# Two layers of graph, mixture and attention on one core: expert rows gathered by a list made on TensorE, results of the second mixture stored in token order

## The chip, the cores and the metric

The kernel runs on one core of a Trainium2 chip. The metric is the device time of one execution in microseconds (us). The core has five engines with queues of their own: TensorE (PE; PEld is its weight load), VectorE (DVE), ScalarE (ACT), GpSimd (POOL) and SyncE (SP), which here only issues DMAs. They pass work to one another through semaphores.

## The reference

3327 tokens of 256 numbers go through two graph layers, two mixtures of experts and one attention; all of it is in f32.

```python
x = x + _L0_gnn_ref(_layernorm(x), adj, W, b)          # (dis * adj * dis) @ x @ W.T + b
x = x + _L0_ffn_ref(_layernorm(x), gate_w, ..., b2)     # top 2 of 8 experts, weighted by softmax
x = x + _L1_gnn_ref(_layernorm(x), adj, W, b)           # the same with relu
x = x + _L1_ffn_ref(_layernorm(x), ln1_g, ..., b2)      # attention, then the second mixture

def _moe(xf, router_w, router_b, w1, b1, w2, b2):       # in _L1_ffn_ref
    probs = jax.nn.softmax(xf @ router_w + router_b, axis=-1)
    _, topk_idx = jax.lax.top_k(probs, TOP_K)
    capacity = int(np.ceil(T * CAPACITY_FACTOR / N_EXPERTS))
    out = jnp.zeros_like(xf)
    for i in range(N_EXPERTS):
        mask = (topk_idx == i).any(-1)
        sel = jnp.sort(jnp.where(mask, tok, T))[:capacity]
        xi = xf[jnp.minimum(sel, T - 1)]
        hi = jax.nn.gelu(xi @ w1[i] + b1[i], approximate=False)
        yi = hi @ w2[i] + b2[i]
        out = out.at[sel].set(yi, mode='drop')          # the last expert that has the token wins
    return out
```

An expert is a product 256 x 1024, a gelu and a product 1024 x 256. In the first mixture every token has two experts, and their outputs are added by their weights. In the second one a token has the output of at most one expert: of its two the one with the higher number that still has room.

## The kernel before

Tokens lie in 26 tiles of 128 (`NT`, padded to `NP` = 3328 rows); a tile is [128 partitions, 256]. `m.x` and `m.xhat` hold x and its normed form in SBUF for all tiles. Large products take f32 operands as two parts, `_hi` (rounded by ScalarE) and `_lo` (the rest, by VectorE), and three passes of TensorE. The program is a row of stages, each a block of its own in which every engine has a queue written out by hand; a stage ends when all its engines have ended.

1. `graph_layer(first=True)`: 182 pieces of the adjacency matrix, by 7 chunks of columns (`CHUNKS`; the first six are 4 tiles wide, the last one 2). A loop runs over positions g; at each, SP loads a piece into `adj_raw`, ScalarE makes `adj_hi` (L410), VectorE `adj_lo` (L636), TensorE multiplies (L570 to L572). The first four chunks run together up to position 103, the others follow one by one. The tail work of chunk c (product by W, normalisation, later products) is spread over positions counted from `turns[c]`, by lists that `at_positions` makes (L246 to L264): positions stand for time here. POOL fills `slots0` and `slots1` with zeroes (27 DMAs, 13.8 MB) in this layer. PE waits for the parameters before its first product (L552).
2. `mixture`: `mixture_routes` makes for each token and choice a slot (`put`, where its row goes) and `get` (where its result lies); slots of one expert are neighbours, in chunks of 256 (`CHUNK`). `mixture_scatter` (L858) sends the normed rows from SBUF to `slots` in DRAM with one indirect DMA a tile and choice on POOL: 52 in the first mixture, 26 in the second. The stage waits for all of them. `expert_layers` (L872) runs over 34 chunks in the first mixture and 20 in the second. SP loads the chunk's rows (L920), both weight matrices (L922, 1 MB each) and biases two chunks ahead; all engines have loops over pairs of chunks. TensorE transposes the rows of the next chunk in the middle of a chunk (`turn`, L937), when rows and weights have arrived; ScalarE and VectorE split rows, weights and hidden values; POOL stores 256 rows of results (L1040), waits until they have landed, and frees the buffer.
3. `graph_layer(first=False)`: the same with further work in its tail: the results of the first mixture are gathered by POOL (L346) and added to x; x of a chunk is normed at `turns[c]` + 8 to + 10 (`roots`, `applies`), but as ScalarE overwrites x, POOL first stores the unnormed x to `x_kept` in DRAM (`keep`), and ScalarE waits for this store (L428's releaser). The order in POOL's queue is: keep(0), then for each chunk c the output bias of c, keep(c + 1), and the q and k stores of the tiles of c (L340). Second normalisation at + 12 to + 14, transposition at + 12, q and k products of a tile (L546, 16 products) and v (L549) at + 13, copied out of PSUM at + 17 by ScalarE. ScalarE's order within a position is the piece's `adj_hi`, then evacuations, roots, applies, and last `taken` and `copied` (`xt`, L439), for which TensorE waits.
4. `attend`: attention by heads.
5. `second_mixture`: normalisation, x loaded back, `gate_logits` (a transposition and a small product for each tile, `transposed_products`), then `mixture` as above, whose last stage `mixture_gather` (L1046) gathers the result of each token with 26 indirect DMAs on POOL and adds it to x with its weight (L1068, 0 where no expert had room). A last stage stores x to `out` in one DMA of 3.4 MB (L1533).

## Time and profile before

| | us |
|---|---|
| median of 3 runs | 2963.14 (2962.2 to 2964.66) |
| profiled execution | 2960.15 |
| its span in the trace | 2958.5 |
| TensorE busy | 2472.5 (84% of the span) |
| VectorE busy | 1993.0 (67%) |
| ScalarE busy | 1573.0 (53%) |
| POOL busy | 1251.6 (42%) |
| routes of the first mixture end | 393.2 |
| first product of its expert loop, its end | 481.7, 889 |
| second graph layer | 891 to 1325 |
| attention | 1326 to 2504 |
| first product of the second expert loop, its end | 2668.9, 2907 |

The stages follow one another, so a saving within one moves all later ones. An engine's busy share of the whole span mixes stages with different limits: the page's second part, the span in 40 slices of 74 us, shows this.

```profile
PE   4789805999997998758999999999999997409992
DVE  5775424888877865438777777777777773328883
ACT  4554304777764543323666666666666665206761
POOL 0001051000004402234888888888888886230003
PEclk9999957999998999876999999999999999559996
```

A digit is the busy share in tenths. Slice 6 (370 to 444 us) is the routes and the scatter: PE 0, POOL 5. Slices 7 to 12 are the first expert loop, 13 to 18 the second graph layer; slices 35 and 36 (PE 4 and 0) hold gates, routes and scatter of the second mixture, and 37 to 39 its expert loop.

### The profile page before, as it was taken

How to read it: one execution, taken by the hardware profiler on the slowest of the kernel's cores; microseconds unless marked ns; L12 is line 12 of the kernel's file. 1: busy time of each engine (PE TensorE's matmuls, PEld its weight loads, DVE VectorE, ACT ScalarE, POOL GpSimd, SP SyncE). 2: the span in 40 equal slices, each digit the busy share in tenths (PEclk: the TensorE clock that was granted, in tenths of full speed). 3: DMA queues.
4: the chain of work that ended last, by engine and by line, in shares of the span. 5: the costliest groups of instructions: out<-in, count | busy, mean ns of one | idle time of the engine just before them, and what ended most of it. 6: DMA issues, size and time to landing. Idle time of an engine off the chain costs nothing. (4 is left out here: it accounts for less than half of the span.)

```text
span 2958.5 us, 54884 instructions
## 1 busy us (share of the span) xinstructions
PE 2472.5 (84%) x20856; PEld 1919.4 (65%) x20856; DVE 1993.0 (67%) x2987; ACT 1573.0 (53%) x2652; POOL 1251.6 (42%) x738
## 2 busy tenths in 40 slices
PE   4789805999997998758999999999999997409992
PEld 3668704999995877644666666666666664409992
DVE  5775424888877865438777777777777773328883
ACT  4554304777764543323666666666666665206761
POOL 0001051000004402234888888888888886230003
PEclk9999957999998999876999999999999999559996
DMA  9988115666646753224000000220000000126663
GB/s 398 362 309 341 47 67 193 230 229 238 240 162 217 235 185 129 97 90 122 14 16 10 14 16 16 46 48 16 10 14 16 10 12 1 46 83 223 241 232 105
DMA packets 118767, 375.96 MB, mean 127 GB/s; under 512 B 22256, under 2 KB 56432, under 8 KB 100656
## 3 DMA queue, kind: packets, MB, share of 16 engines
q1 hardware_dynamic: 96192, 302.78, 28.9%
q0 software_dynamic: 20800, 65.82, 6.0%
q10 hardware_dynamic: 1584, 4.75, 0.4%
q8 instruction: 129, 2.11, 0.3%
q14 instruction: 62, 0.51, 0.1%
HBM read 314.30 MB, written 58.98 MB: 126 GB/s over the span
## 5 line engine op out<-in xcount | busy, mean ns | idle before, releaser
L1255 POOL TENSOR_TENSOR at_pool_sum<-at_pool_sum,at_probs 128x1024 f32<-128x1024 f32 x364 | 866.7, 2381 | 97.0 <-ACT at_probs L1381 55.7
L1410 DVE TENSOR_REDUCE at_part_max<-ps_x 128x2 f32<-128x1024 f32 x624 | 734.4, 1221 | 228.1 <-PE ps_x L1311 227.8
L1381 ACT ACTIVATE at_probs<-ps_s 128x512 f32<-128x512 f32 x1352 | 698.4, 603 | 323.3 <-PE ps_s L1270 292.8
L1270 PE MATMUL ps_s<-at_qst,at_kst 97*128 97x256 f32 x2704 | 517.6, 311 | 5.2 <-ACT at_probs L1381 4.0
L1270 PEld LDWEIGHTS ps_s<-at_qst,at_kst 97*128 97x128 f32 x2704 | 368.9, 189 | 218.5 <-ACT at_probs L1381 127.2
L1287 PE MATMUL ps_oz<-at_probs,k_xhat 128*32 128x256 f32 (+1 forms) x5408 | 391.4, 386 | 0.0
L570 PE MATMUL ps_acc<-adj_hi,y_hi 128*128 128x512 f32 (+1 forms) x728 | 290.1, 399 | 93.6 <-DMA k_bias<-bias 32.8
L636 DVE TENSOR_TENSOR adj_lo<-adj_raw,adj_hi 128x1024 fp32r<-128x1024 f32 (+1 forms) x182 | 208.7, 1148 | 184.1 <-ACT adj_hi L410 181.7
L1040 POOL DMA_DIRECT2D results<-ex_res x54 | 39.3, 727 | 645.4 <-DVE ex_res L1027 645.4
L571 PE MATMUL ps_acc<-adj_lo,y_hi 128*128 128x512 f32 (+1 forms) x728 | 278.1, 382 | 0.0
L572 PE MATMUL ps_acc<-adj_hi,y_lo 128*128 128x512 f32 (+1 forms) x728 | 277.9, 382 | 0.0
L991 ACT ACTIVATE ex_hid<-ps_ex_h,ex_b 128x256 f32<-128x256 f32 x432 | 197.7, 476 | 128.3 <-PE ps_ex_h L943 115.1
L1009 DVE TENSOR_TENSOR ex_w_lo<-ex_w,ex_w_hi 128x2048 fp32r<-128x2048 f32 x108 | 242.7, 2289 | 33.5 <-ACT ex_w_hi L981 33.5
L941 PE MATMUL ps_ex_h<-ex_rt_hi,ex_w_hi 128*128 128x256 f32 x864 | 246.1, 285 | 9.8 <-DVE ex_w_lo L1009 9.8
L941 PE MATMUL ps_ex_o<-ex_w_hi,ex_hid_hi 128*128 128x256 f32 x864 | 246.7, 286 | 0.0
L943 PE MATMUL ps_ex_h<-ex_rt_hi,ex_w_lo 128*128 128x256 f32 x864 | 243.2, 282 | 0.0
L942 PE MATMUL ps_ex_h<-ex_rt_lo,ex_w_hi 128*128 128x256 f32 x864 | 243.0, 281 | 0.0
L942 PE MATMUL ps_ex_o<-ex_w_lo,ex_hid_hi 128*128 128x256 f32 x864 | 242.4, 281 | 0.0
L943 PE MATMUL ps_ex_o<-ex_w_hi,ex_hid_lo 128*128 128x256 f32 x864 | 242.3, 280 | 0.0
L410 ACT ACTIVATE adj_hi<-adj_raw 128x1024 fp32r<-128x1024 f32 (+1 forms) x182 | 174.9, 988 | 104.4 <-PE ps_acc L572 104.0
L570 PEld LDWEIGHTS ps_acc<-adj_hi,y_hi 128*128 128x128 f32 x728 | 140.6, 193 | 127.9 <-issue 70.5
L1311 PE MATMUL ps_x<-at_keys,at_queries 32*128 32x512 f32 x1248 | 191.0, 509 | 27.3 <-DMA at_keys<-qk_parts 13.2
(201 smaller groups left out, 4047.6 us busy)
## 6 DMA issues: line engine op xcount, KB each, us to landing
ex_w<-w SPq DMA_DIRECT2D x108, 1024.0 KB, 6.8
adj_raw<-adjT SPq DMA_DIRECT2D x156, 512.0 KB, 4.9
k_xhat<-adj SPq DMA_DIRECT2D x26, 1664.0 KB, 8.6
slots<-zeros POOLq DMA_DIRECT2D x27, 512.0 KB, 24.2
ex_rows<-slots SPq DMA_DIRECT2D x54, 256.0 KB, 2.9
results<-ex_res POOLq DMA_DIRECT2D x54, 256.0 KB, 2.8
at_qst<-qk_parts SPq DMA_DIRECT2D x78, 128.0 KB, 2.5
ex_b<-b SPq DMA_DIRECT2D x54, 128.0 KB, 2.1
```

The lines of the kernel that those rows point to most:

```text
L570: pe.matmul(out, y_hi[:, k, cols], hi[:, g % PIECE_RING, at], start=k == 0, stop=False)
L571: pe.matmul(out, y_hi[:, k, cols], lo[:, g % PIECE_RING, at], start=False, stop=False)
L572: last = pe.matmul(out, y_lo[:, k, cols], hi[:, g % PIECE_RING, at], start=False, stop=k == NT - 1)
L941: pe.matmul(out, hi, by_hi, start=start, stop=False)
L942: pe.matmul(out, hi, by_lo, start=False, stop=False)
L943: return pe.matmul(out, lo, by_hi, start=False, stop=stop)
L1009: dve.tensor_tensor(w_lo[:, k, layer, :], w[:, k, layer, :], w_hi[:, k, layer, :].bitcast(F32), ALU.subtract).then_inc(weights_lo, 1)
L1255: pool.tensor_tensor(pool_sum[:, g % 2], pool_sum[:, g % 2], probs[:, tile % RING], ALU.add).then_inc(pool_added, 1)
L1270: last = pe.matmul(ps_s[:, unit % S_BANKS, hh, :], kst[:, 2 * j + hh, k * P:(k + 1) * P], qst[:, g % 2, 2 * j + hh, :], start=True, stop=True)
L1287: last = pe.matmul(ps_oz[h * DK:(h + 1) * DK, 0, :], m.xhat[0:rows, k, (hg * FOUR + h) * DK:(hg * FOUR + h + 1) * DK], probs[0:rows, tile ...
L1381: act.activation(probs[:, tile % RING, 2 * j:2 * j + 2], ps_s[:, unit % S_BANKS], ACT.Exp, scale=scale).then_inc(taken, 1)
L1410: dve.tensor_reduce(part_max[:, g % 2, heads, qt, kc], ps_x[:, pair, :], AX.X, ALU.max).then_inc(x_free, 1)
```

## The change

1. Rows and lists. The normed rows go to DRAM in token order (`rows_d`): in the first layer chunk by chunk on POOL behind `normed`, in the second mixture in one DMA on SP within `transposed_products`. `mixture_scatter`, `slots0`, `slots1` and their zeroes are gone; instead the part of `results1` that holds tokens is zeroed (13 DMAs, 3.4 MB).
2. `expert_layers` first makes a list of the token in each slot. VectorE splits `put` into column (`put >> 7`) and lane (`put & 127`), marks both as one-hot rows of bf16 (`col_hot`, `lane_hot`) in two groups, and multiplies the columns by the tile number; ScalarE scales them by the lane. TensorE sums the products over all marks (`find_rows`: 52 marks and 68 columns for the first mixture, 26 and 40 for the second), which gives the token at each (lane, column). VectorE makes `index` of it (`list_rows`).
3. POOL gathers the rows of a chunk with two indirect DMAs (`fetch`, two chunks ahead of the store) in place of SP's load; `turn` waits only for these rows. SP's weight loads of chunks 0 and 1 wait for counts of `weights_lo` that now come in two steps, the second after the list. POOL's loop is written out.
4. In the second mixture (`SPREAD`) two indirect DMAs store a chunk's results in token order (`place`; slots without a token go to rows of their own). `mixture_gather` and the last stage become `mixture_output`: SP loads the results in 7 groups, VectorE adds, ScalarE stores 7 groups of `out`.
5. Second graph layer: the store of x to `x_kept` goes from POOL to SP, at `turns[c]` + 11, with two semaphores in turn; `applies` is at + 13 and all that follows it three positions later. For both layers ScalarE's `taken` and `copied` come ahead of evacuations, roots and applies within a position, and the roots are numbered by their positions (`norm`). The wait for the parameters goes from TensorE's start to its first product by W.

```diff
+        @block.sync
+        def _(sp):
+            sp.dma_start(rows.rearrange("(k p) d -> p k d", p=P), src[:]).then_inc(rows_kept, 16)
+            sp.wait_ge(rows_kept, 16)
...
-    applies = at_positions([(at + 10 + q, p) for at, c, p, q in pairs])
-    roots2_begin, roots2_end = at_positions([(turns[c] + 12, c) for c in range(CHUNKS)]), at_positions([(turns[c] + 13, c) for c in range(CHUNKS)])
-    applies2 = at_positions([(at + 14 + q, p) for at, c, p, q in pairs])
+    applies = at_positions([(at + (10 if first else 13) + q, p) for at, c, p, q in pairs])
+    keeps = at_positions([(turns[c] + 11, c) for c in range(CHUNKS)])
+    roots2_begin, roots2_end = at_positions([(turns[c] + 15, c) for c in range(CHUNKS)]), at_positions([(turns[c] + 16, c) for c in range(CHUNKS)])
+    applies2 = at_positions([(at + 17 + q, p) for at, c, p, q in pairs])
+    norms = sorted((turns[c] + (15 if second else 8), second, c) for c in range(CHUNKS) for second in range(1 if first else 2))
+    norm = {(c, second): n for n, (_, second, c) in enumerate(norms)}
...
-        turned_at = at_positions([(at + 12 + 3 * q, p) for at, c, p, q in pairs])
-        copied_at = at_positions([(at + 16 + 3 * q, p) for at, c, p, q in pairs])
-        produced_at = at_positions([(at + 13 + 3 * q + i, 2 * p + i) for at, c, p, q in pairs for i in range(2)])
-        taken_at = at_positions([(at + 17 + 3 * q + i, 2 * p + i) for at, c, p, q in pairs for i in range(2)])
-        split_at = at_positions([(at + 18 + 3 * q + i, 2 * p + i) for at, c, p, q in pairs for i in range(2)])
+        turned_at = at_positions([(at + 15 + 3 * q, p) for at, c, p, q in pairs])
+        copied_at = at_positions([(at + 19 + 3 * q, p) for at, c, p, q in pairs])
+        produced_at = at_positions([(at + 16 + 3 * q + i, 2 * p + i) for at, c, p, q in pairs for i in range(2)])
+        taken_at = at_positions([(at + 20 + 3 * q + i, 2 * p + i) for at, c, p, q in pairs for i in range(2)])
+        split_at = at_positions([(at + 21 + 3 * q + i, 2 * p + i) for at, c, p, q in pairs for i in range(2)])
...
-                done = 0
-                for slots, chunks in ((m.slots0, MOE0_CHUNKS), (m.slots1, MOE1_CHUNKS)):
-                    cols = chunks * CHUNK // P * D
-                    view = slots[0:chunks * CHUNK, :].rearrange("(p n) d -> p (n d)", p=P)
-                    for n in range(0, cols, ZERO_COLS):
-                        width = min(ZERO_COLS, cols - n)
-                        pool.dma_start(view[:, n:n + width], zeros[:, 0:width]).then_inc(cleared, 16)
-                        done += 16
-                pool.wait_ge(cleared, done)
+                for n in range(0, NT, ZERO_TILES):
+                    pool.dma_start(m.results1[0:NP, :].rearrange("(p n) d -> p n d", p=P)[:, n:n + ZERO_TILES, :], zeros[:]).then_inc(rows_kept, 16)
+                for c in range(CHUNKS):
+                    at = slice(first_tile(c), first_tile(c + 1))
+                    pool.wait_ge(normed, at.stop)
+                    pool.dma_start(m.rows_d[at.start * P:at.stop * P, :].rearrange("(k p) d -> p k d", p=P), m.xhat[:, at, :]).then_inc(rows_kept, 16)
+                pool.wait_ge(rows_kept, 16 * (CHUNKS + NT // ZERO_TILES))
...
-            keep(0)
             for c in range(CHUNKS):
...
-                if c + 1 < CHUNKS:
-                    keep(c + 1)
...
+            def keep(c):
+                at = slice(first_tile(c), first_tile(c + 1))
+                sp.wait_ge(chain, at.stop)
+                sp.dma_start(m.x_kept[:, at.start * D:at.stop * D], m.x[:, at, :].rearrange("p t d -> p (t d)")).then_inc(x_kept[c % 2], 16)
...
+                if not first:
+                    for c in keeps(g):
+                        keep(c)
...
+                for n in taken_at(g):
+                    take_logits(n) if first else round_product(n)
+                for p in copied_at(g):
+                    copy_turned(p)
...
-                        act.wait_ge(x_kept, 16 * c + 16)
-                        apply(p, m.x, m.x, normed, 2 * c + 1)
+                        act.wait_ge(x_kept[c % 2], c // 2 * 16 + 16)
+                        apply(p, m.x, m.x, normed, norm[c, 0] + 1)
...
+                elif first:
+                    pe.wait_ge(params_loaded, 16 * 7)
...
-                    sp.dma_start(rows[:, k], slots[ds(i * 2 * CHUNK + k * CHUNK, CHUNK), :].rearrange("(a p) d -> p a d", p=P)).then_inc(loaded[k], 16)
...
-            eng.wait_ge(loaded[k], n * 24 + (48 - 24 * k))
+            eng.wait_ge(loaded[k], n * 16 + (32 - 16 * k))
...
+            def find_rows():
+                for i in range(MARKS):
+                    if i % GROUP == 0:
+                        pe.wait_ge(planes_made, i // GROUP + 1)
+                        pe.wait_ge(lanes_made, i // GROUP + 1)
+                    last = pe.matmul(ps_o[:, 0, 0:2 * COLS], lane_hot[:, i, :], planes[:, i].rearrange("p a n -> p (a n)"),
+                                     start=i == 0, stop=i == MARKS - 1)
+                last.then_inc(found, 1)
+
             def turn(n, k):
-                arrived(pe, n, k)
+                pe.wait_ge(rows_come[k], n * 16 + (32 - 16 * k))
...
+            def lanes():
+                for g in range(MARKS // GROUP):
+                    act.wait_ge(matched, g + 1)
+                    at = slice(g * GROUP, (g + 1) * GROUP)
+                    act.activation(planes[:, at, 0, :], col_hot[:, at, :], ACT.Copy, scale=lane[:, 0:1]).then_inc(lanes_made, 1)
+
+            lanes()
...
-            dve.sem_inc(weights_lo, 4)
+            dve.sem_inc(weights_lo, 2)
...
+            def mark_rows():
+                c = Count(coded)
+                put = m.put[:, 0:n_rows, :].rearrange("p a k -> p (a k)")
+                c.inc(dve.tensor_scalar(code_i[:, 0], put, 7, None, ALU.arith_shift_right))
+                c.inc(dve.tensor_scalar(code_i[:, 1], put, P - 1, None, ALU.bitwise_and))
+                c.inc(dve.tensor_scalar(lane[:], m.token_f[:, 0:1], 1.0 if SPREAD else 0.0, None, ALU.add))
+                c.settle(dve)
+                c.inc(dve.tensor_copy(code[:], code_i[:]))
+                c.settle(dve)
+                for g in range(MARKS // GROUP):
+                    at = slice(g * GROUP, (g + 1) * GROUP)
+
+                    def along(a, n):
+                        return a.rearrange("p (i b) -> p i b", b=1).broadcast_to([P, GROUP, n])
+
+                    def numbers(n):
+                        return m.iota_b[:, 0:n].rearrange("p (b n) -> p b n", b=1).broadcast_to([P, GROUP, n])
+
+                    dve.tensor_tensor(col_hot[:, at, :], along(code[:, 0, at], COLS), numbers(COLS), ALU.is_equal).then_inc(matched, 1)
+                    dve.tensor_tensor(lane_hot[:, at, :], along(code[:, 1, at], P), numbers(P), ALU.is_equal)
+                    dve.wait_ge(matched, g + 1)
+                    tile = g * GROUP % NT
+                    dve.tensor_tensor(planes[:, at, 1, :], col_hot[:, at, :], along(m.iota_b[:, tile:tile + GROUP], COLS), ALU.mult).then_inc(planes_made, 1)
+
+            def list_rows():
+                dve.wait_ge(found, 1)
+                dve.tensor_copy(slot_of[:].rearrange("p a n -> p (a n)"), ps_o[:, 0, 0:2 * COLS]).then_inc(coded, 1)
+                dve.wait_ge(coded, 5)
...
+                if not SPREAD:
+                    dve.scalar_tensor_tensor(index[:], slot_of[:, 1], float(P), slot_of[:, 0], ALU.mult, ALU.add).then_inc(listed, 1)
+                    return
...
+                dve.tensor_scalar(index[:], slot_of[:, 0], -1.0, 0.0, ALU.add, ALU.max).then_inc(listed, 1)
...
+                c.inc(dve.scalar_tensor_tensor(place[:], slot_of[:, 0], -1.0, slot_of[:, 1], ALU.add, ALU.add))
...
+            mark_rows()
+            list_rows()
+            dve.sem_inc(weights_lo, 2)
...
+            def fetch(n):
+                if n >= 2:
+                    pool.wait_ge(turned, n - 1)
+                for a in range(TT):
+                    pool.indirect_dma_start(out=rows[:, n % 2, a, :], out_offset=None, in_=m.rows_d,
+                                            in_offset=bass.IndirectOffsetOnAxis(index[:, TT * n + a:TT * n + a + 1], 0)).then_inc(rows_come[n % 2], 16)
+
+            def store(n):
+                k = n % 2
+                pool.wait_ge(out_made, n + 3)
+                if SPREAD:
+                    for a in range(TT):
+                        pool.indirect_dma_start(out=results, out_offset=bass.IndirectOffsetOnAxis(place[:, TT * n + a:TT * n + a + 1], 0),
+                                                in_=res[:, k, a, :], in_offset=None).then_inc(stored[k], 16)
+                    pool.wait_ge(stored[k], n // 2 * 32 + 32)
+                else:
+                    pool.dma_start(results[n * CHUNK:(n + 1) * CHUNK, :].rearrange("(a p) d -> p a d", p=P), res[:, k]).then_inc(stored[k], 16)
+                    pool.wait_ge(stored[k], n // 2 * 16 + 16)
+                pool.sem_inc(res_free, 1)
+
             pool.sem_inc(res_free, 2)
-            with pool.Fori(0, chunks // 2) as i:
-                for k in range(2):
-                    n = i * 2 + k
-                    pool.wait_ge(out_made, n + 3)
-                    pool.dma_start(results[ds(i * 2 * CHUNK + k * CHUNK, CHUNK), :].rearrange("(a p) d -> p a d", p=P),
-                                   res[:, k]).then_inc(stored[k], 16)
-                    pool.wait_ge(stored[k], i * 16 + 16)
-                    pool.sem_inc(res_free, 1)
+            pool.wait_ge(listed, 1)
+            fetch(0)
+            fetch(1)
+            if SPREAD:
+                pool.wait_ge(listed, 2)
+            for n in range(chunks):
+                if n + 2 < chunks:
+                    fetch(n + 2)
+                store(n)
...
+                sp.dma_start(got[:, at, :], results[at.start * P:at.stop * P, :].rearrange("(k p) d -> p k d", p=P)).then_inc(come[c], 16)
...
+                for k in chunk_tiles(c):
+                    dve.scalar_tensor_tensor(x[:, k, :], got[:, k, :], weight[:, k:k + 1], x[:, k, :], ALU.mult, ALU.add).then_inc(added, 1)
+
+        @block.scalar
+        def _(act):
+            for c in range(CHUNKS):
+                at = slice(first_tile(c), first_tile(c + 1))
+                act.wait_ge(added, at.stop)
+                act.dma_start(out[:, at, :], x[:, at, :]).then_inc(put, 16)
+            act.wait_ge(put, 16 * CHUNKS)
```

## Rows read from the trace of the kernel before

**Rows 1.** Windows: us, busy of PE, PEld, DVE, ACT, POOL; clock, DMA, GB/s
```profile
482.00:890.00 408.00, 401.52 (x3396) 401.09 (x3396) 340.61 (x406) 282.32 (x387) 24.85 (x34) 0.99 0.58 218
1094.00:1268.00 174.00, 137.65 (x796) 122.60 (x794) 90.14 (x248) 60.77 (x111) 39.85 (x44) 0.89 0.31 114
2669.00:2912.00 243.00, 236.98 (x1996) 236.62 (x1996) 199.25 (x238) 164.07 (x226) 14.41 (x20) 0.98 0.56 207
```

**Rows 2.** Timeline at the first scatter: start, us, engine, line, tiles [idle before <-releaser]
```profile
392.99 0.18 DVE L836 TENSOR_SCALAR k_get<-rt_best 128x26 int32<-128x26 f32 x1
394.42 1.05 POOL L867 DMA_INDIRECT slots<-k_xhat,mx_put  x1 [152.73 <-PEq L861]
...
459.18 0.96 POOL L867 DMA_INDIRECT slots<-k_xhat,mx_put  x1 [0.30 <-issue]
...
475.71 0.72 PEld L937 LDWEIGHTS ps_ex_t<-k_ident,ex_rows 128*128 128x128 f32 x4 [96.46 <-DMA ex_w<-w]
...
481.72 0.58 PE L941 MATMUL ps_ex_h<-ex_rt_hi,ex_w_hi 128*128 128x256 f32 x1 [4.89 <-DVE ex_w_lo L1009]
```

**Rows 3.** The page's groups: busy, mean ns of one, idle before and its releaser
```profile
L1009 DVE TENSOR_TENSOR ex_w_lo<-ex_w,ex_w_hi 128x2048 fp32r<-128x2048 f32 x108 | 242.7, 2289 | 33.5 <-ACT ex_w_hi L981 33.5
...
L1019 DVE CAST ex_hid_hi<-ex_hid 128x512 fp32r<-128x512 f32 x216 | 94.6, 438 | 53.8 <-ACT ex_hid L991 51.9
```

**Rows 4.** DMAs, median us to landing, from 882 to 925 and from 2900
```profile
k_xhat<-results,k_get POOLq DMA_INDIRECT x15, 4.7
...
got<-results,k_get POOLq DMA_INDIRECT x26, 2.8
```

**Rows 5.** Timeline between the routes and the second expert loop
```profile
2616.24 1.07 POOL L867 DMA_INDIRECT slots<-k_xhat,mx_put  x1 [64.94 <-PEq L861]
...
2654.30 0.42 SPq L920 DMA_DIRECT2D ex_rows<-slots  x1
...
2668.89 0.58 PE L941 MATMUL ps_ex_h<-ex_rt_hi,ex_w_hi 128*128 128x256 f32 x1 [4.89 <-DVE ex_w_lo L1009]
```

**Rows 6.** Waits from 1094 to 1262 (total, times, longest), then timeline there
```profile
ACT k_x L428 <- DMA x_kept<-k_x: 38.7, 5, 8.9
...
PE ps_acc L546 <- ACT xt L439: 34.7, 7, 8.7
...
1125.10 0.75 DVE L650 SCALAR_TENSOR_TENSOR k_x<-gnn_tmp,k_x 128x256 f32<-128x256 f32 x2
...
1140.36 0.57 POOL L329 DMA_DIRECT2D x_kept<-k_x  x1
...
1145.35 3.58 PE L546 MATMUL ps_acc<-xt,wqk 128*128 128x128 f32 x16 [7.17 <-ACT xt L439]
...
1256.69 3.78 PE L546 MATMUL ps_acc<-xt,wqk 128*128 128x128 f32 x16 [8.72 <-ACT xt L439]
```

**Rows 7.** Timeline of TensorE behind the last piece of the second graph layer
```profile
1270.06 2.05 PE L546 MATMUL ps_acc<-xt,wqk 128*128 128x128 f32 x16
...
1274.19 2.02 PE L546 MATMUL ps_acc<-xt,wqk 128*128 128x128 f32 x16 [1.21 <-DVE qk_lo L673]
```

**Rows 8.** The end: timeline, the output's DMA (size, landing), the additions' group
```profile
2907.43 0.73 POOL L1040 DMA_DIRECT2D results<-ex_res  x1 [9.27 <-DVE ex_res L1027]
...
2912.88 1.01 POOL L1059 DMA_INDIRECT got<-results,k_get  x1 [4.72 <-PEq L1051]
...
out<-k_x SPq DMA_DIRECT2D x1, 3328.0 KB, 9.3
...
L1068 DVE SCALAR_TENSOR_TENSOR k_x<-got,k_weight,k_x 128x256 f32<-128x256 f32 x26 | 12.6, 484 | 28.6 <-DMA got<-results,k_get 28.6
```

**Rows 9.** Timeline: a long gather, and VectorE beside it
```profile
912.24 2.54 DVE L636 TENSOR_TENSOR adj_lo<-adj_raw,adj_hi 128x1024 fp32r<-128x1024 f32 x2
...
912.45 1.83 POOL L346 DMA_INDIRECT k_xhat<-results,k_get  x1 [0.30 <-issue]
```

**Rows 10.** Timeline of TensorE early in the first layer
```profile
53.28 0.76 PE L570 MATMUL ps_acc<-adj_hi,y_hi 128*128 128x512 f32 x1 [3.27 <-ACT adj_hi L410]
```

170 lines of the change are left out of this document (77 added, 93 removed).

## The prediction

> **What bounds the kernel now.** I read the times by stretch first [rows 1]. From 482 to 890 us, the 34 expert chunks of the first mixture, TensorE is busy 401.5 of 408 us at full clock: TensorE is the bound there, and nothing that is only moved in or out of this loop changes the time. The same is true of the 20 chunks of the second mixture. Three kinds of stretch are different: before each of these loops TensorE does nothing for 54 to 88 us; from 1094 to 1268 us, the second half of the second graph layer, it is busy 137.7 of 174 us at a granted clock of 0.89; and after 2912 us it does nothing at all. The change touches all of these, so I priced each by the order of time in its own stretch, then looked at which wait ends last.
>
> The hole before the first loop [rows 2]: the routes end at 393.17 us; POOL issues 52 scatters, one each 1.27 us, from 394.42 to 460.14; TensorE turns the first rows at 475.71 (it waits for rows and weights together) and multiplies at 481.72. The hole is a chain: 66 us of issuing, 15.6 us in which the last scatter lands, the stage closes and SP loads, and 6.0 us of preparing the first operands. The second mixture has the same chain with 26 scatters [rows 5].
>
> In the second graph layer ScalarE waits 38.7 us, five times, for the store of x to `x_kept`, and TensorE waits 34.7 us behind it for `xt` [rows 6]. One instance: x of a chunk is final at 1125.85 (L650), but POOL issues the store at 1140.36, behind the q/k stores of the chunk before and its bias addition; ScalarE goes on when it has landed. So the store is late because of its place in POOL's queue, not because it is slow.
>
> **Part 1: the first list.** The scatters, their landing and the closing of their stage go. The chain that replaces them, from the end of the routes at 393.17: 1.25 us to open the stage (as before the first scatter); the small operations on codes, some six of 0.2 us, 1.2; then two groups of three VectorE products over 26 marks each, of 1768, 3328 and 1768 elements per partition. A row of 2048 elements shows 1.12 ns an element, a copying row 0.86 [rows 3]; I take 1.1 for these, so 7.5 us a group, 15.0 in all. No row has 2-byte operands of this kind; the copying row bounds it at 11.8 from below, and half as much again, 22.5, is my bound above, since broadcast operands may cost more. ScalarE's planes (1768 elements) and the first 26 products on TensorE lie beside this; behind it are the last 26 products, priced by four transposes at low clock, 0.72 us, as 0.18 each [rows 2]: 4.7 (3.0 at full clock). Reading the sums and making the index: 0.8. Then POOL: two gathers for the first chunk, the second issued 1.3 us after the first; gathers landed in 4.7 us at the median beside other loads and 2.8 alone [rows 4]. SP starts the weights of chunk 1 (2 MB) in this same moment, so I take 4.7, together 6.0. From the turn to the first product stays 6.0. The weights of chunk 0 load under the list. Sum: 1.25 + 1.2 + 15.0 + 4.7 + 0.8 + 6.0 + 6.0 = 35.0, so the loop starts at 428.1 and not at 481.72: 53.6 saved (43 to 61).
>
> The Trainium skill (VectorE: DVE Perf Modes, What auto-detection actually checks) says that an operation of two sources runs at double rate if every tensor has 2-byte elements at step 1; each product here has an operand that repeats one element, which by it keeps the single rate. No row here shows either; at the double rate, an estimate by that page, both lists together would save 10 us more.
>
> **Part 2: the second list.** Only 26 marks and 40 columns: groups of 520, 1664 and 520 elements, 3.2 us each. From the end of the routes at 2615.0 (the first scatter starts 1.2 later, as in the first mixture) [rows 5]: 1.25 + 1.2 + 6.4 + 13 products 2.3 + sums and index 1.0 + gathers 6.0 + 6.0 = 24.2, so 2639.2 against 2668.89: 29.7 saved (24 to 33). The further operations that make `place` lie beside the gathers.
>
> **Part 3: the loops.** SP loses the load of rows, POOL gets two gathers a chunk, and in the second mixture two scatters for one store. POOL waits in order for turn n, for the result of chunk n and for its landing; queued behind that is only the gather for n + 3, needed over 12 us later. POOL's own time a chunk is at most 2 x 1.3 + 2 x 1.3 + 2.8 of landing = 8 us, of 11.8 that a chunk takes. Cost 0, up to 8 in all for one late row at the start. The turn no longer waits for weights, but TensorE has no idle time here that this could give back.
>
> **Part 4: the end.** Before: last store issued at 2907.43, first gather at 2912.88, 26 gathers one by one, then the output in one piece of 3.4 MB that takes 9.3 us to land, and the end at 2958.5 [rows 8]. After: two scatters for the last chunk, of which the second ends near 2909.7 (issued 1.3 after 2907.4, 1.0 long); at the start of the second loop 26 scatters of 1.27 us end near 2649.1 and SP loads at 2654.30, 5.2 later [rows 5], so SP issues its first load of results near 2915. Then 3.4 MB in and 3.4 MB out, in seven groups; 26 additions of 0.48 us [rows 8], 12.5, lie under it. At the 366 GB/s of the output (3.4 MB in 9.3 us) both ways take 18.6 us, less some overlap of their latencies; end near 2934.5. Saved: 24 (17, if the groups of 1 KB rows run at two thirds of this rate, to 29).
>
> **Part 5: the second graph layer.** SP issues the store at position +11 of the turn, when x is final at +8, and ScalarE needs it at +13. It lands before that, so the wait goes. SP waits for `chain` with the loads of the next pieces behind it; it runs up to four pieces ahead and the ring holds four, so this costs nothing as long as x comes within one position. Of the seven gaps of TensorE five are long and hold 33.5 us; two of these stand in [rows 6]. The 16 products after such a gap take 3.58 and 3.78 us, while 16 that follow close on others take 2.05 [rows 7]: some 1.6 more each time, 8.2 in all, from the lower clock. What is late next is TensorE itself, whose own work fills the rest. Against it: the second half of each chunk is three positions later, so two more tiles fall behind the last piece, where a tile takes 4.1 us (from 1270.06 to 1274.19, as q, k and v of one tile wait for the lift of the one before [rows 7]) in place of the 2.85 of its products: 2.5. I allow 2 for new small waits. Saved 37 (15 to 42).
>
> **Parts that cost or give nothing.** The wait for the parameters leaves the start of the first layer, but what TensorE won there it would lose at once: at 53.28 it has waited 3.27 us for ScalarE's `adj_hi` [rows 10]; 0. Zeroes are 3.4 MB in place of 13.8, beside a bound TensorE; 0. Stores of `rows_d` in the first layer lie under the last tile but for some 0.5; those of the second mixture have 31 us of gate products over them. The order on ScalarE moves the first layer's tail by a microsecond either way. Together 0, within 3.
>
> **Sum.** 53.6 + 29.7 + 24 + 37 = 144.3. The profiled execution took 2960.15 us (a span of 2958.5 and 1.65 around it), so 2815.9; it stands 3 us under the median of 2963.14, so the median comes to 2818.8.
>
> **Rivals.** (a) The gap in the second graph layer takes another name. ScalarE and VectorE hand each piece and each tile to one another; with the later positions one of these hand-overs, or the longer tail, may take what the store gives back. It speaks against this that VectorE is busy only 90 of 174 us there [rows 1]. Then Part 5 gives 0 to 10 for 37, 5 in the middle: 2851. (b) The lists or the end are cheaper than taken: the double rate, landings of 2.8 us, TensorE at full clock: 53.6 becomes 61, 29.7 becomes 33 and 24 becomes 28, 14.7 more: 2804. (c) Slower than before: POOL's address work for the gathers blocks VectorE. One gather lasted 1.83 us for the usual 0.95, while VectorE ran two subtractions [rows 9]. If it is VectorE that stands still for as long, it loses 3.7 us a chunk in the first loop and 7.4 in the second. It is busy 340.6 of 408 us there [rows 1], so it has 2.0 us a chunk to spare, and the loops grow by 1.7 x 34 and 5.4 x 20, 166 us in all: 2985. It decides the sign once VectorE loses more than 4.7 us a chunk on average (its 2.0 to spare and 144.3 / 54). Against it: the two subtractions beside that gather took 2.54 us, as everywhere else. The Trainium skill (SBUF — State Buffer, Who interferes with whom) has this rule: a VectorE instruction with two inputs in SBUF and a POOL instruction that reads SBUF block each other, whoever comes first. The trace shows only POOL's side of it. (d) The gathers come late in each chunk, because stores and scatters hold POOL: at four operations of 1.83 us, 0.3 between them and 4.7 of landing a chunk takes 13.2 us in the second loop, 1.4 x 20 = 28 more: 2847.
>
> **How the numbers follow.** Forecast 0.61 (2819, by its own bounds 2800 to 2838), (a) 0.15, (b) 0.14, (c) 0.04, (d) 0.06. The range 2792 to 2856 holds the first, (b) and most of (a) and (d). A measurement of this kernel tells about 0.2%, 6 us, from no change. Faster by more 0.96; the 0.04 of (c) are 0.03 slower and 0.01 within, where its price is about that which decides.
>
> **What would show it.** In the profile after: the first product of the first loop about 35 us after the end of the routes, of the second 24; the product lines on VectorE near 3.65 and 1.9 us in the first list; no wait of ScalarE for `x_kept`; TensorE over 95% busy from 1094 us (less what is saved) to the last piece, with a tail a little longer than 58 us; 11.8 us a chunk in both loops; and some 20 us from the first load of results to the end. It is wrong if chunks take longer, if ScalarE's wait comes back under `k_shift` or `xt`, or if the list's long products take twice their price.

## The result, and the profile after

The changed kernel takes 2854.3 us (median of 4 runs, 2850.7 to 2859.9) against 2963.6 for the kernel before: the ratio is 0.9633 (0.9616 to 0.9650), 109 us saved. I had forecast 2819 and a saving of 144. (One of the four executions of `e5_old_positions`, 3538.3 us at a granted clock of 0.64, was slow and is left out of its time below.) The profiled execution has a span of 2851.7 us for 2958.5, so 106.8 us are to be placed. This table is made from the two timelines, each stretch between the same two events (the second graph layer runs from TensorE's last product of the first loop to its last product of the layer):

| stretch | before | after | saved | forecast |
|---|---|---|---|---|
| start to the end of the first routes | 393.2 | 390.9 | 2.3 | 0 |
| to the first product of the first expert loop | 88.6 | 33.2 | 55.4 | 53.6 |
| first expert loop | 401.8 | 402.8 | -1.0 | 0 |
| second graph layer | 433.0 | 413.2 | 19.8 | 37 |
| attention, gates and routes | 1298.5 | 1298.8 | -0.3 | 0 |
| to the first product of the second loop | 53.8 | 24.8 | 29.0 | 29.7 |
| second loop, to its last issue of results | 238.5 | 257.6 | -19.1 | -1.3 |
| from there to the end | 51.1 | 30.5 | 20.6 | 25.3 |

(In the last two rows the forecast's second scatter of the last chunk, 1.3 us, is put with the loop, where the table has it.) Both lists came out as worked out. The miss of 37.5 us in the sum is in three places: the second graph layer, the second loop and, with 4.7, the end.

The first list in the timeline of the kernel after, which answers to [rows 2] (start, us, engine, line, tiles, idle before and its releaser):

```profile
392.43 1.08 DVE L1050 TENSOR_TENSOR ex_hid<-ex_code,k_iota_b 128x884 bf16<-128x884 bf16 x1
393.42 1.89 DVE L1051 TENSOR_TENSOR ex_w<-ex_code,k_iota_b 128x1664 bf16<-128x1664 bf16 x1
...
395.22 1.07 DVE L1054 TENSOR_TENSOR k_xhat<-ex_hid,k_iota_b 128x884 bf16<-128x884 bf16 x1
...
407.70 1.66 PE L941 MATMUL ps_ex_o<-k_xhat,ex_w 128*128 128x136 bf16 x13 [2.13 <-DVE k_xhat L1054]
...
410.24 1.05 POOL L1107 DMA_INDIRECT ex_rows<-moe_rows,ex_index  x1 [48.02 <-DVE ex_index L1061]
...
418.08 1.12 PE L949 MATMUL ps_ex_t<-k_ident,ex_rows 128*128 128x128 f32 x4 [8.73 <-DMA ex_rows<-moe_rows,ex_index]
```

The marks come in four groups of 13 and not, as I wrote, in two of 26 (the second list has two of 13); the number of elements is the same. VectorE is busy with them from 392.43 to 407.6, 15.2 us for the 15.0 of the sum. The 1664 elements in 1.89 us are 1.13 ns each, at 2 bytes as at 4. The last products on TensorE took 1.66 us and not 4.7, but the first rows are turned 7.8 us behind the first gather, not 6.0; the two cancel.

In the second loop the chunks no longer come every 11.8 us. POOL's timeline over one cycle:

```profile
2601.26 1.38 POOL L1107 DMA_INDIRECT ex_rows<-moe_rows,ex_index  x1 [6.64 <-DMA results<-ex_res,ex_place]
2602.95 0.96 POOL L1107 DMA_INDIRECT ex_rows<-moe_rows,ex_index  x1 [0.30 <-issue]
2604.21 1.00 POOL L1115 DMA_INDIRECT results<-ex_res,ex_place  x1 [0.30 <-issue]
2605.52 0.99 POOL L1115 DMA_INDIRECT results<-ex_res,ex_place  x1 [0.30 <-issue]
2613.50 0.98 POOL L1107 DMA_INDIRECT ex_rows<-moe_rows,ex_index  x1 [7.00 <-DMA results<-ex_res,ex_place]
```

and the waits there (2564 to 2820 us; total, times, longest), the first and the third of which the kernel before does not have:

```profile
POOL ex_rows L1107 <- DMA results<-ex_res,ex_place: 114.8, 17, 7.9
POOL results L1115 <- DVE ex_res L1095: 36.9, 5, 17.6
...
PE ps_ex_t L949 <- DMA ex_rows<-moe_rows,ex_index: 15.1, 8, 3.5
```

Two gathers, two scatters and 7 us of waiting until the scatters have landed make 12.2 us here, more than a chunk's 11.8. From the first gather at 2588.27 to the one at 2793.86 sixteen cycles take 12.85 us on average (10.9 to 14.8), since the first gather of a cycle takes up to 2.80 us and the wait up to 7.9; seventeen such cycles, each 1.05 us over 11.8, make 17.9 of the 19.1 us that the loop grew. POOL is the bound: it waits for VectorE's results only five times in twenty chunks.

In the second graph layer the wait for `x_kept` [rows 6] is gone, and TensorE is busy 124.7 of 140 us at a clock of 0.96 from 1037 to 1177, for 137.7 of 174 at 0.89 [rows 1]. But three gaps of 3.2 to 4.0 us are new. One of them, with what stands ahead of it:

```profile
1122.62 3.62 DVE L643 TENSOR_TENSOR adj_lo<-adj_raw,adj_hi 128x512 fp32r<-128x512 f32 x1 [1.11 <-ACT adj_hi L419]
...
1123.31 2.38 POOL L336 TENSOR_TENSOR k_x<-k_x,k_rows 128x1024 f32<-128x1024 f32 x1
...
1128.61 0.68 DVE L680 TENSOR_TENSOR qk_lo<-ps_acc,k_cols 128x512 f32<-128x512 f32 x1
...
1129.43 3.41 PE L555 MATMUL ps_acc<-xt,wqk 128*128 128x128 f32 x16 [3.96 <-DVE qk_lo L680]
```

A subtraction of VectorE that takes 0.69 us elsewhere takes 3.62, and while it runs POOL adds the output bias to x. The lift of a tile out of PSUM (L680) is late by as much, and TensorE waits for that, then takes 3.41 us for sixteen products, at a granted clock of 0.56, near the lower of its two levels (1.2 and 2.4 GHz). The two other gaps have the same pair of lines (additions at 1087.70 and 1154.56): the subtractions beside them take 4.28 us (128x1024, 1.23 elsewhere) and 3.64.

The end, which answers to [rows 8]:

```profile
2821.23 0.97 POOL L1115 DMA_INDIRECT results<-ex_res,ex_place  x1 [0.30 <-issue]
...
2830.55 5.78 SPq L1146 DMA_DIRECT2D got<-results  x7
...
2848.41 0.88 DVE L1153 SCALAR_TENSOR_TENSOR k_x<-got,k_weight,k_x 128x256 f32<-128x256 f32 x2 [1.30 <-DMA got<-results]
```

9.3 us lie between the last scatter's issue and SP's first load, and 21.2 from there to the end.

### The profile page after: what moved, and what is told of

It is laid out like the page before. It is cut to its first block and busy times, and to the rows that moved or that the text cites. A ratio compares the mean times of both kernels' runs of the same rounds, so it can differ in the third digit from the quotient of the medians.

```text
span 2851.7 us, 54629 instructions
## 1 busy us (share of the span) xinstructions
PE 2484.0 (87%) x20934; PEld 1927.4 (68%) x20934; DVE 2026.2 (71%) x3022; ACT 1577.8 (55%) x2658; POOL 1299.9 (46%) x749
## 5 line engine op out<-in xcount | busy, mean ns | idle before, releaser
L643 DVE TENSOR_TENSOR adj_lo<-adj_raw,adj_hi 128x1024 fp32r<-128x1024 f32 (+1 forms) x182 | 217.5, 1197 | 163.5 <-ACT adj_hi L419 161.3
L1107 POOL DMA_INDIRECT ex_rows<-moe_rows,ex_index x108 | 124.7, 1155 | 369.0 <-DMA results<-ex_res,ex_place 114.8
L1029 DVE TENSOR_TENSOR ex_w_lo<-ex_w,ex_w_hi 128x2048 fp32r<-128x2048 f32 x108 | 242.7, 2289 | 38.5 <-ACT ex_w_hi L994 38.5
L577 PEld LDWEIGHTS ps_acc<-adj_hi,y_hi 128*128 128x128 f32 x728 | 140.7, 193 | 124.7 <-issue 99.8
```

What stands on the lines that cost most here:

```text
L577: pe.matmul(out, y_hi[:, k, cols], hi[:, g % PIECE_RING, at], start=k == 0, stop=False)
L1029: dve.tensor_tensor(w_lo[:, k, layer, :], w[:, k, layer, :], w_hi[:, k, layer, :].bitcast(F32), ALU.subtract).then_inc(weights_lo, 1)
```

## The experiments

### The second loop

Theory: the landing of the scatters, waited for ahead of the next gathers, makes POOL the bound. Rival: the gathers land late for other reasons, or VectorE is slowed. `e1_free_later` moves only the wait (and the release of the buffer behind it):

```diff
-                    pool.wait_ge(stored[k], n // 2 * 32 + 32)
-                pool.sem_inc(res_free, 1)
...
                 if n + 2 < chunks:
                     fetch(n + 2)
+                if n:
+                    free(n - 1)
                 store(n)
+            free(chunks - 1)
```

> The kernel after, with one change in the order of POOL's queue in the expert loops: the wait for the landing of a chunk's results now stands behind the gathers of the next chunk, not ahead of them. In the kernel after, POOL's cycle in the second loop is two gathers, two scatters and 6.6 to 7.7 us of waiting for the scatters' landing, 12.3 to 12.6 us against 11.8 us of TensorE's work. Theory (POOL's queue is the bound there, because the landing is waited for in order): the second loop, from its first product to its last result store, falls from 256.3 to about 239 us, no wait of TensorE for ex_rows is left, and the whole takes about 2837. Rival (gathers land late for other reasons, such as sharing the DMA engines with the weights, or VectorE is slowed by POOL): the loop stays within 3 us of 256. The first loop and all other stretches stay within 1 us in both.

2834.5 us (2832.5 to 2837.9; ratio 0.9566, 0.9551 to 0.9582), 20 under the kernel after. The second loop takes 239.0 us for 257.6, as in the kernel before; TensorE waits nowhere for `ex_rows`, and POOL waits for VectorE's results at every chunk:

```profile
POOL results L1115 <- DVE ex_res L1095: 144.7, 20, 17.5
```

`e8_plain_stores` takes the scatters away and leaves POOL's order:

```diff
-                    for a in range(TT):
-                        pool.indirect_dma_start(out=results, out_offset=bass.IndirectOffsetOnAxis(place[...], 0), ...)
-                    pool.wait_ge(stored[k], n // 2 * 32 + 32)
+                    pool.dma_start(results[n * CHUNK:(n + 1) * CHUNK, :]..., res[:, k]).then_inc(stored[k], 16)
+                    pool.wait_ge(stored[k], n // 2 * 16 + 16)
```

> The kernel after, with the results of the second mixture stored in the order of slots by one plain DMA a chunk (the output's last addition then takes other tokens' rows: this part is left out). It takes the scatters away and leaves the gathers and the order of POOL's queue. Theory: POOL's cycle falls to two gathers, a store and a landing of 3.3 us, under 9 us, so the second loop takes 239 us, the same as with e1_free_later. If the gathers themselves held the loop it would stay above 250. At the end, if the scatters are what makes the step to the last stage longer, SP's first load comes 4.7 us behind the last store's issue, as between the first expert loop and the second graph layer; if not, it stays at 9.3.

2833.3 us in the one run, and the loop takes 238.8. So the gathers alone don't hold the loop: it needs the scatters and the order of the wait together.

The two kinds of store can't be compared by their landings as they stand, 7.0 us for the scatters and 3.2 for these plain stores: in e8 every store that has weight loads near it goes out 1.6 to 2.4 us ahead of them. In the kernel after, POOL's wait has pushed the scatters to the moment at which SP starts the 2 MB:

```profile
2604.21 1.00 POOL L1115 DMA_INDIRECT results<-ex_res,ex_place  x1 [0.30 <-issue]
2604.32 0.81 SPq L925 DMA_DIRECT2D ex_w<-w  x2
2605.52 0.99 POOL L1115 DMA_INDIRECT results<-ex_res,ex_place  x1 [0.30 <-issue]
```

Of its forty scatters five go out 1.4 to 2.0 us ahead of the weight loads and land in 2.8 to 3.2 us; the 29 that go out between 0.7 us ahead and 0.8 behind land in 5.0 to 8.6; the six behind the last weights land in 2.4 to 3.4. So a scatter lands late when it goes out with the weights. In e1 the first scatter of a chunk goes out 1.6 to 2.0 us ahead of them and the second 0.3 to 0.7. That a plain store would be quicker at the later moment is not shown.

At the end of e8, SP's first load comes 7.8 us behind the last store's issue, between the 4.7 and the 9.3 of the two expectations: 1.5 us go with the scatters, the rest does not (one trace each).

### The second graph layer

`e2_no_bias` replaces POOL's addition by a bare count of its semaphore:

```diff
-                pool.tensor_tensor(m.x[:, at, :], m.x[:, at, :], m.rows[:, 5:6, :].broadcast_to(...), ALU.add).then_inc(biased, 1)
+                pool.sem_inc(biased, 1)
```

> The kernel after, without the addition of the output bias to x on POOL in the second graph layer: this part of the computation is left out, so x lacks the bias from there on. In the kernel after, two subtractions of VectorE that take 0.69 us elsewhere take 3.62 and 3.64 us, each just when POOL's addition of 2.4 us runs, and TensorE then waits 3.2 to 4.0 us for VectorE three times. Theory (VectorE stands still while POOL adds): these three waits of 11 us in all and the slow products behind them go; the stretch from the first product of the layer to its last falls from 388.5 to some 375, and no 512-wide subtraction is over 0.8 us. Rival (the hand-over between ScalarE and VectorE at these positions is the cause, with the later positions of the change): the waits for qk_lo stay at 3 to 4 us and the layer within 3 us of 388.5.

2843.9 us in the one run. From the first to the last product the layer takes 375.5 us for 388.5. The three gaps are gone, no subtraction of VectorE is stretched (the longest of L642 takes 1.23 us), and of the waits for the lift only short ones are left, six of them ahead of the last piece with 3.1 us in all:

```profile
PE ps_acc L554 <- DVE qk_lo L679: 9.2, 11, 1.2
```

In the kernel after, the same wait is 17.7 us in 10 times, the longest 4.0. The hand-over between ScalarE and VectorE, my rival (a), is not the cause.

`e3_both` keeps the whole computation and takes both causes away: the order of e1, and the bias added by VectorE.

```diff
-                add_output_bias(c)
...
+    biases = at_positions([(turns[c] + 19, c) for c in range(CHUNKS)])
...
+                    for c in biases(g):
+                        add_output_bias(c)
+                dve.tensor_tensor(m.x[:, at, :], m.x[:, at, :], m.rows[:, 5:6, :].broadcast_to(...), ALU.add).then_inc(biased, 1)
```

> A complete kernel: the order of POOL's queue of e1_free_later, and the output bias added by VectorE (at position +19 of a chunk's turn) in place of POOL. By the first two theories: about 17 us from the second expert loop and 10 to 14 from the second graph layer, less up to 1.3 us for each of seven additions that VectorE now carries where it is waited for; about 2825 (2820 to 2832). By both rivals: 2850 to 2860.

2822.4 us (2822.1 to 2826.2; ratio 0.9528, 0.9512 to 0.9544), 32 under the kernel after. The layer takes 397.8 us for 413.2, the second loop 240.0 for 257.6.

`e4_part5_alone` puts the layer's part of the change alone into the kernel before (the `keep` on SP, the later positions, ScalarE's order, the place of the wait for the parameters: those lines of the diff above).

> The kernel before, with the second graph layer's part of the change alone: the store of x on SP at +11, all that follows at three positions later, ScalarE's order within a position, and the place of the wait for the parameters. If this part is independent of the others, it gives what the comparison of the two traces shows for it: some 19 us in the second graph layer and 1 to 3 in the first, so about 2942. If the lighter traffic or the other changed stages had a hand in it, it gives less than 15.

2941.3 us (2935.9 to 2941.8; ratio 0.9926, 0.9910 to 0.9943). The layer takes 412.1 us, 20.9 under the kernel before, and the first routes end at 390.3: this part doesn't depend on the others.

`e5_old_positions` leaves the store of x on SP, and sets the positions back:

```diff
-    applies = at_positions([(at + (10 if first else 13) + q, p) for at, c, p, q in pairs])
-    keeps = at_positions([(turns[c] + 11, c) for c in range(CHUNKS)])
+    applies = at_positions([(at + 10 + q, p) for at, c, p, q in pairs])
+    keeps = at_positions([(turns[c] + 8, c) for c in range(CHUNKS)])
...
-        turned_at = at_positions([(at + 15 + 3 * q, p) for at, c, p, q in pairs])
+        turned_at = at_positions([(at + 12 + 3 * q, p) for at, c, p, q in pairs])
```

> The kernel after, with the store of x to x_kept on SP (at +8, where x is final) but with the positions of the kernel before: applies at +10, second roots at +12, transposition at +12, products at +13. It tells the store's move from POOL to SP from the three later positions. Theory A (the place in POOL's queue was the cause): most of the gain stays; ScalarE waits for x_kept for up to 2.5 us at a time where it waited 8; the second graph layer loses less than 6 us against the kernel after, and its tail behind the last piece has 8 tiles and not 10, so it is some 8 to 13 us shorter. Theory B (the positions carry the gain): ScalarE's wait for x_kept comes back at 4 us or more a time, and the layer is 8 us or more slower than in the kernel after.

2842.4 us (2841.5 to 2847.1; ratio 0.9597, 0.9578 to 0.9617). ScalarE has no wait for `x_kept` left even so (the expectation of e9 below says that these waits came back in part: the trace has none). From the layer's first product to the last piece it takes 332.6 us for 325.6, and behind it 50.9 for 62.9: the layer is 5.1 us shorter than in the kernel after (408.1 for 413.2), and 1.6 and 5.0 shorter than in e8 and e7, which ran on the same chip with this layer as in the kernel after. So the store's place in a queue carried the gain, and the later positions gave nothing here; their tail cost more than they brought. (The rest of the difference to the kernel after is in the second loop, 251.7 us here; it lies between 251.7 and 260.5 in the kernels that keep the scatters and this order on POOL.)

`e6_old_act_order` sets ScalarE's order back in both layers (`taken` and `copied` last).

> The kernel after, with ScalarE's taken and copied last within a position, as before, in both graph layers. I gave this part nothing, within 3 us. If it is so, the time is within 3 us of the kernel after. If the first layer's 3.7 us of earlier end and part of the second layer's gain come from it, it is 4 us or more slower, with TensorE's waits for xt in the second graph layer grown.

2850.5 us (2844.2 to 2853.7; ratio 0.9611, 0.9595 to 0.9628): its interval overlaps that of the kernel after. In the traces the second layer is shorter (405.6 us, where kernels with this layer's code unchanged have 409.7 to 413.2), and the first routes end later (394.5, where others have 390.2 to 393.7). The sizes are too near to that spread to be called shown.

### The end

`e7_end_one_piece` has one load, all additions and one store:

```diff
-            for c in range(CHUNKS):
-                sp.dma_start(got[:, at, :], results[at.start * P:at.stop * P, :]...).then_inc(come[c], 16)
+            sp.dma_start(got[:], results[0:NP, :].rearrange("(k p) d -> p k d", p=P)).then_inc(come[0], 16)
```

> The kernel after, with the last stage in one load, all additions and one store in place of seven groups each. If the stage is bound by the bytes that the DMA engines move, groups give only the additions and one latency: from SP's first load to the end it takes 9.3 for the load, 12.5 for the additions of 26 tiles on VectorE that now stand alone, and 9.3 for the store, some 32 us in place of 21.2, so 10 to 12 us slower. If the groups disturb one another (the last of the seven loads took 13.2 us to land), it is slower by less than 8.

2864.0 us (2861.7 to 2871.3; ratio 0.9668, 0.9648 to 0.9688), 10 slower. The timeline gives the size of each part:

```profile
2831.17 0.38 SPq L1144 DMA_DIRECT2D got<-results  x1
2843.76 10.38 DVE L1151 SCALAR_TENSOR_TENSOR k_x<-got,k_weight,k_x 128x256 f32<-128x256 f32 x26 [23.47 <-DMA got<-results]
2854.17 0.36 ACTq L1156 DMA_DIRECT2D out<-k_x  x1
```

12.6 us for the load, 10.4 for the additions, 9.7 for the store (it lands after 9.3, and the span ends 0.4 later), 32.7 in all. The load and the landing of the store are 21.9 together, and the seven groups took 21.2 with the additions among them. So the groups hide the additions and almost nothing of the transfers. The DMA engines are busy 97% of the time from 2830.5 to 2848.4 us in the kernel after: the bytes are the bound.

### Putting them together

`e9_all_old_positions` is e3_both with the old positions (the bias at +16).

> e3_both with the old positions in the second graph layer (store of x on SP at +8, applies at +10, transposition at +12, products at +13, the bias on VectorE at +16). If the gains add up: the old positions gave 5.1 us in the second graph layer (adjacency phase 7.0 longer, tail 12.0 shorter), and with POOL's additions gone the phase is expected no worse, so 5 to 8 us under e3_both's 2822.4: about 2816. If the waits for x_kept, which came back in part, were hidden until now under POOL's additions, it gains less than 3.

`e10_split_order` is e9 with ScalarE's new order in the first layer and the old one in the second. `e11_split_new_positions` is e3_both with that split, at the later positions.

> e9_all_old_positions with ScalarE's order within a position as in the change in the first graph layer and as in the kernel before in the second. With the old order in both layers the first layer was 3.6 us longer and the second 7.6 shorter. If this is a property of the two layers, it gains up to 7 us on e9, so about 2810; if it was tied to POOL's additions or to the later positions, it is within 2 us of e9 or slower.

> e3_both with the same split of ScalarE's order, and the later positions of the change. By the 7.6 us that the old order gave in the second layer at these positions: 2815. If the gain came from what stood beside POOL's additions, it stays within 3 us of e3_both's 2822.4. Against e10 it shows what the positions are worth once the other two causes are gone.

All three missed: 2848.0, 2854.3 and 2843.8 us (ratios 0.9605, 0.9618, 0.9589). The stages show where:

| | first loop | second graph layer | second loop |
|---|---|---|---|
| e3_both | 401.7 | 397.8 | 240.0 |
| e9_all_old_positions | 409.6 | 399.5 | 255.5 |
| e10_split_order | 409.2 | 405.3 | 261.5 |
| e11_split_new_positions | 410.2 | 395.4 | 251.5 |

No edit of these three touches the loops, yet they are 8 and 12 to 22 us longer. In all three ScalarE starts late behind TensorE once a chunk; e11's ScalarE at the end of a first half of a chunk:

```profile
577.34 0.47 ACT L1020 ACTIVATE ex_hid<-ps_ex_h,ex_b 128x256 f32<-128x256 f32 x1 [1.00 <-PE ps_ex_h L964]
577.71 0.59 ACT L1000 ACTIVATE ex_rt_hi<-ps_ex_t 128x512 fp32r<-128x512 f32 x1
```

TensorE turned the rows at 576.29, so ScalarE follows by 1.42 us, where all other kernels have 0.64 at the median in this loop. The delay begins one operation earlier: TensorE's product for the `ex_hid` above ends at 576.45, and ScalarE starts it at 577.34. The three had run in one job on one chip. So e11 ran once more, unchanged, in another job on another chip:

> The same kernel as e11_split_new_positions, run once more, in another job. That job's three kernels all had longer expert loops (409.2 to 410.2 us for the first, against 401.5 to 402.8 in all others; 251.5 to 261.5 for the second, against 239.0 and 240.0 with the same POOL order in e1 and e3), although none of their edits touches these loops, and the kernel before, run beside them, took 2965.9 as elsewhere. If this belongs to the place of that job, this run has loops of 402 and 240 us and comes to 2818 to 2824, its second graph layer of 395 us being 2.4 shorter than in e3_both. If it belongs to the kernel (its code lies otherwise), the loops stay at 410 and 250 and it comes to 2840 or more.

2819.6 us (2817.9 to 2821.4; ratio 0.9524, 0.9509 to 0.9538), with loops of 402.5 and 240.2 us, the layer at 395.6, and the rows taken over again at once:

```profile
574.25 0.60 PE L958 MATMUL ps_ex_t<-k_ident,ex_rows 128*128 128x128 f32 x4
...
574.89 0.60 ACT L1000 ACTIVATE ex_rt_hi<-ps_ex_t 128x512 fp32r<-128x512 f32 x1
```

The same kernel took 2843.8 us in the one job and 2819.6 in the other, while the kernel before took 2965.9 and 2961.3 in these jobs. The longer loops belong to the place (the chip, or something else that came with that job: each was used once), not to the edits. Why ScalarE wakes later there, and why the kernel before hardly suffers, stays open.

Within the second graph layer, e9, e10 and e11 can still be set beside e3, since the kernel of e11 and e12 takes 395.4 us there on the one chip and 395.6 on the other: without POOL's additions the old positions are no better than the later ones (399.5 against 397.8), and the split order makes little difference at the later positions (395.5 against 397.8). At the old positions it does: e10 takes 5.8 us more than e9 on the same chip, and 9.9 more than e11, which differs in the positions alone. So with the old order of ScalarE the later positions are worth some 10 us, and with the new one 1.7; each is one trace. The ratios of this kernel and of e3_both, 0.9524 and 0.9528, lie within each other's intervals: both are some 33 us faster than the kernel after, and they are not told apart.

## Why the prediction was right, and where it failed

The direction and the range held, the range by luck: 2854.3 lies 1.7 us inside its upper end of 2856 and 16 above the forecast's own bounds (2800 to 2838). It reached so far up for the sake of rivals (a) and (d), and a part of each came true: other waits in the second layer, and a POOL that is late in the second loop. The likeliest value was 35 us too low, and one of the prediction's own signs of being wrong, "if chunks take longer", came true in the second loop. By its own steps:

**Parts 1 and 2, the lists: right.** 55.4 and 29.0 us for 53.6 and 29.7. The price per element from the row of 2048 elements [rows 3] held at 1.13 ns. The Trainium skill (VectorE: DVE Perf Modes, What auto-detection actually checks) gives the double rate only where every tensor is 16-bit at step 1, and by that rule these products with a repeated operand keep the single one: the trace agrees. The products on TensorE were mis-sized (1.66 us for 4.7), and so was the way from the gather to the turn (7.8 for 6.0). The second list's 3.2 us a group are not its price per element, which gives 3.0, as measured (2540.34 to 2543.37).

**Part 3, the loops: wrong, and this is the failed step that cost most.** "POOL's own time a chunk is at most 2 x 1.3 + 2 x 1.3 + 2.8 of landing = 8 us". The 2.8 us are the landing of gathers with no other traffic [rows 4], and that of the plain stores in the loops before, which go out some 2 us ahead of the weights. In the loop the forty scatters landed in 7.0 us at the median, most of them issued with the 2 MB of weights, and the last four in 2.4 to 2.6, when nothing else ran. In Part 1 I had taken the loaded value for the gathers from [rows 4] (4.7) and here, for the same kind of transfer in the same traffic, the idle one. With 7.0 the prediction's own sum gives a cycle of 12.2 us; measured are 12.85, as its gathers were also longer than 1.3. Rival (d) was the right mechanism: it priced the loop's growth at 28 us, where it grew 19.1, with longer instructions and a shorter landing than there were, and I gave it 0.06. e1 and e8 show it from two sides.

**Rival (c): not seen in the loops.** VectorE's long subtraction takes 2289 ns there before and after [rows 3]. POOL's gathers took 1155 ns on average (1380 in the second loop, up to 2802) for the 954 of the last gathers before: POOL's address work is what stretches. Of the 26 that had no subtraction of two SBUF operands beside them none took over 1.05 us.

**Part 5, the second graph layer: right for the wait, wrong for what came next.** I put the wait and its slow products at 41.7 us less 2 for small new waits. Between the layer's first product and the last piece the two traces differ by 32.5 us, of which 5.7 are the products of two tiles that now stand behind: 26.8 are real. The missing 13 are what e2 gives back when POOL's addition goes. "What is late next is TensorE itself" was wrong: next was VectorE, standing still for POOL. What would have told it stood in the trace: the kernel before has these additions too, at 1138.07, 1178.01 and 1214.38, in the middle of ScalarE's waits for `x_kept`, where VectorE had nothing to do. The wait that was removed had been their cover. One addition before that fell on a working VectorE shows the price:

```profile
1096.80 2.40 POOL L334 TENSOR_TENSOR k_x<-k_x,k_rows 128x1024 f32<-128x1024 f32 x1 [22.36 <-ACT k_xhat L428]
...
1096.93 2.28 DVE L104 TENSOR_TENSOR k_shift<-k_shift,k_guarded 128x4 f32<-128x4 f32 x1
```

An operation of 4 elements took 2.28 us for 0.16. The Trainium skill (SBUF — State Buffer, Who interferes with whom) says that a VectorE instruction with two inputs in SBUF contends with a GpSimd instruction that reads SBUF. I used that rule for the gathers, where VectorE didn't suffer, and not for the addition, where the trace agrees with it: every operation of two SBUF inputs that had more than 0.2 us in common with an addition was stretched (the four above, and `k_x<-gnn_tmp,k_x` at 1048.37 in the kernel after, 1.80 us for 0.37), and those with an input from PSUM were not (0.48 us at 1047.58 in the kernel after, 0.68 at 1283.06 in the one before).

**The tail: right in kind, mis-sized.** Two more tiles behind the last piece cost 13.7 us less the 5.7 of their products, 8.0 for 2.5. I read the step within a pair of tiles, 4.1 us [rows 7]; but the tiles come in pairs, and from one pair's first products to the next pair's it takes 10.6 us (1182.38 to 1192.95), as the next pair waits for its transposition to be copied by ScalarE. A gap of 2.3 us at 1177.6 and products at the lower clock are the rest.

**Part 4, the end: right in kind, 4.7 us short.** Its own terms end at 2915 + 18.6 = 2933.6, not 2934.5. It took 9.3 us from the last scatter's issue to SP's load and not the 6.2 I took from the second loop's start. In the kernel before this step took 7.6 us from the end of the last scatter in the first mixture and 5.2 in the second; I took the shorter. What it consists of isn't settled: e8 puts 1.5 us on the scatters, and the DMA engines moved nothing from 2824 to 2830.5. The transfers took 21.2 for 19.5.

**The parts at nothing** held within 2.3 us, about as much as that point moves between kernels with the same first layer (390.2 to 393.7).

## What to carry to other kernels

When a wait goes, look at what ran under it, on every engine: work that was free there is priced anew, and here a cheap addition of POOL then held up VectorE and through it TensorE for 13 us. Put a wait for a transfer's landing behind everything in its queue that others need sooner, and take the landing from rows under the same traffic, issued at the same moment of it: here 1.4 us ahead of the weight loads or with them made 3 us or 7. One kernel measured 24 us apart in two places: run the winner again elsewhere.

## What the runs showed of the hardware

A row scatter of 128 rows of 1 KB landed in 2.4 us alone, in 2.8 to 3.2 when it went out 1.4 to 2.0 us ahead of the 2 MB of weight loads, and in 5.0 to 8.6 when it went out with them. A plain store of 256 KB, seen near the loads only 1.6 to 2.4 us ahead of them, took 3.2 or 3.3 at the median with gathers in the same queue, 2.8 in the kernel before. VectorE's subtraction of 512 elements took 3.62 and 3.64 us beside POOL's addition of 2.4 us, 0.69 otherwise. With loads and stores of 512 KB going at once, 3.4 MB in and 3.4 MB out took 21.2 us (322 GB/s), where one after the other they took 21.9: going both ways at once gained next to nothing. And in one job, on one chip, ScalarE followed TensorE 0.8 us later, once a chunk, in three kernels, one of which did not do so elsewhere.
